# Attention a: matmuls of pairs of heads, and a GpSimd mask by minimum times 2^62

## The reference, cut to what matters

```python
topk = max(1, int(Tx * 0.3))                       # 76 of 256 keys
scores = jnp.einsum('bhid,bhjd->bhij', q, k) * scale   # 16 heads of 8
topk_scores, indices = jax.lax.top_k(scores, topk)
masked = jnp.full_like(scores, -jnp.inf).at[bi, hi, ti, indices].set(topk_scores)
attn = jax.nn.softmax(masked, axis=-1)
out = jnp.einsum('bhij,bhjd->bhid', attn, v)
```

## Time and profile before

| | |
|---|---|
| median of 3 runs | 5576.79 us (5576.01 to 5579.73) |
| profiled execution | 5576.97 us, span 5575.2 us |
| TensorE matmul busy | 5186.2 us (93%), 34686 instructions |
| VectorE busy | 4103.8 us (74%) |
| ScalarE busy | 3163.3 us (57%) |
| GpSimd busy | 2558.4 us (46%) |
| mean granted TensorE clock | 0.816 of 2.4 GHz |

### The profile page before, as it was taken

How to read it: one execution, slowest core, us unless ns; L and a number is a source line. 1 busy time by engine, 2 the same in 40 slices (tenths; PEclk the granted TensorE clock), 3 DMA queues, 4 the chain that set the end, 5 groups by cost and what they waited for, 6 DMA issues and landing times. The chain is left out here.

```text
span 5575.2 us, 122336 instructions
## 1 busy us (share of the span) xinstructions
PE 5186.2 (93%) x34686; PEld 3325.6 (60%) x34686; DVE 4103.8 (74%) x14487; ACT 3163.3 (57%) x10145; POOL 2558.4 (46%) x3026
## 2 busy tenths in 40 slices
PE   4699999999997999999989999989999999999998
PEld 3344444444443444444458888866666666788887
DVE  3788888888878888888748888855554554788886
ACT  3577777777776777777512222247766776222222
POOL 1466665665655665665534444421111111444444
PEclk6666666666666666666579999999999999999999
DMA  2000000000000000000023434310000000444344
GB/s 66 10 13 10 10 13 10 13 10 9 13 10 10 10 13 9 13 10 10 7 47 82 86 81 87 79 35 11 11 10 10 12 10 8 88 81 86 82 85 99
DMA packets 358603, 188.74 MB, mean 34 GB/s; under 512 B 190691, under 2 KB 346886, under 8 KB 358150
## 3 DMA queue, kind: packets, MB, share of 16 engines
q1 hardware_dynamic: 358150, 183.55, 16.3%
HBM read 147.04 MB, written 11.01 MB: 28 GB/s over the span
## 5 line engine op out<-in xcount | busy, mean ns | idle before, releaser
L831 ACT ACTIVATE junk<-SS,nt 128x256 bf16<-128x256 f32 x3072 | 1515.8, 499 | 79.7 <-DVE SS L946 45.1
L496 POOL TENSOR_SCALAR gone<-SS,mid 128x256 bf16<-128x256 f32 x1024 | 1228.6, 1200 | 457.4 <-DVEq L1024 326.0
L1188 POOL TENSOR_TENSOR f_hid<-f_g_m,f_cbs 128x256 f32<-128x256 f32 x1024 | 743.6, 726 | 850.5 <-DVE f_g_m L1433 661.7
L1288 ACT ACTIVATE f_th<-bank 128x256 f32<-128x256 f32 x1088 | 417.0, 383 | 1146.7 <-PE bank L1219 1146.7
L668 PE MATMUL bank<-q4x,k4x 32*128 32x256 f32 x2048 | 999.1, 579 | 0.0
L641 PE MATMUL bank<-k,q 32*128 32x256 f32 x2048 | 803.9, 584 | 40.6 <-DVE SS L946 40.6
L688 PE MATMUL bank<-pT,vaug 128*32 128x256 f32 x2048 | 830.3, 553 | 0.5 <-ACT pT L817 0.5
L1218 PE MATMUL bank<-f_xTf,wgT 128*128 128x256 f32 x2176 | 691.8, 400 | 52.6 <-DVE f_g_m L1433 37.0
L1834 DVE TENSOR_REDUCE nmxb<-bank 128x2 f32<-128x512 f32 x512 | 330.1, 688 | 475.5 <-PE bank L1606 475.5
L817 ACT ACTIVATE pT<-bank 128x512 f32<-128x512 f32 x512 | 301.4, 589 | 628.8 <-PE bank L675 626.1
L1219 PE MATMUL bank<-f_xTf,wuT 128*128 128x256 f32 x2176 | 650.9, 381 | 0.0
(11 more groups left out here) (233 smaller groups left out, 8295.7 us busy)
## 6 DMA issues: line engine op xcount, KB each, us to landing
f_cbs<-f_shares SPq DMA_DIRECT2D x512, 256.0 KB, 5.8
q4x<-q SPq DMA_DIRECT2D x64, 256.0 KB, 2.3
k4x<-k SPq DMA_DIRECT2D x64, 128.0 KB, 2.1
qrow<-q_rows SPq DMA_DIRECT2D x512, 8.0 KB
q_rows<-qTb SPq DMA_DIRECT2D x32, 128.0 KB, 1.7
out_dram<-xres SPq DMA_DIRECT2D x4, 1024.0 KB, 9.3
q4x<-nmx_rows SPq DMA_DIRECT2D x128, 4.0 KB
f_shares<-f_combT SPq DMA_DIRECT2D x64, 32.0 KB, 1.4
```

The lines of the kernel that those rows point to most:

```text
L496: last = pool.tensor_scalar(gone[:, h % 4, i, :], SS[:, (u - lag) % 4, c, :], mid[:, (u - lag) % 4, c:c + 1], FAR, ALU.is_lt, ALU.mult)
L831: nc.scalar.activation(junk[:, c % 2, :], SS[:, uu % 4, c, :], ACT.Sign, bias=bias(c), accum_out=acc[:, k, uu % 4, c:c + 1]).then_inc(s["s ...
L1188: pool.tensor_tensor(hid[:, e % NBUF, :], g_m[:, e % NBUF, :], cbs[:, par, e, :], ALU.mult).then_inc(s["hid"], 1)
```

## The change

TensorE's loop over eight places becomes a loop over four pairs of heads. `PAIRS` replaces `stage`: pairs 0 to 2 are heads 2 and 3, 4 and 5, 6 and 7 of group t-3, pair 3 is heads 0 and 1 of group t-2. For each half the pair's two masks come first, then the scores of two heads (2d+2 and 2d+3; none for pair 3), then both heads' remove. After both halves comes the work of M0 or M1, then `weigh` of the same pair, alternating between its heads. ScalarE makes the two exponentials of a pair together, at every second place. pT has four buffers instead of two, and `pv` counts pairs.

GpSimd computes min(score - mid, 0) instead of (score < mid) times 1e20, and the diagonal that TensorE multiplies with is 2^62 instead of -1. GpSimd masks two heads before the second `move` and two behind it (three and none before). `gram`, `qtok` and `mom` go from bank M1 to M0, `ktok` is made in the even step, `oT` goes to M1. `normalise` moves from place 6 to place 0 of the next step, `check_flags` from 3 to 4.

```diff
-        USES = ({"v": 0, "xT": -1, "q0": -1, "q1": -1, "k": -1, "qn": -1, "oT": 2},
-                {"f0": 1, "n0": 2, "ktok": -1, "qtok": -1, "f1": 1, "gram": -1, "mom": -1, "n1": 1, "y": 2})
+        USES = ({"v": 0, "xT": -1, "q0": -1, "q1": -1, "k": -1, "qn": -1, "gram": -1, "qtok": -1, "mom": -1},
+                {"f0": 1, "ktok": -1, "n0": 2, "oT": 2, "f1": 1, "y": 2, "n1": 1})
...
+        PAIRS = ((3, 2), (3, 4), (3, 6), (2, 0))
...
-                                last = pool.tensor_scalar(gone[:, h % 4, i, :], SS[...], mid[...], FAR, ALU.is_lt, ALU.mult)
+                                last = pool.tensor_scalar(gone[:, h % 4, i, :], SS[...], mid[...], 0.0, ALU.subtract, ALU.min)
...
-                    outsiders(2, (0, 1, 2))
+                    outsiders(2, (0, 1))
                     if runs(t):
                         move(1, "u2", nt[:, 0, :], nt[:, 1, :])
+                    outsiders(2, (2, 3))
                     if not even and ahead:
                         guess(bb + 1, (par + 1) % 2)
-                    outsiders(2, (3, 4, 5))
+                    outsiders(2, (4, 5))
...
+                    for d in range(4):
+
+                        late, a = PAIRS[d]
+                        g, v = t - late, (u - late) % 4
+                        ahead = d < 3 and runs(t, -1)
+                        n = 2 * d + 2
                         if ahead:
-                            free_bank(t + 1, h + 2)
+                            free_bank(t + 1, n + 1)
+                        if runs(g):
+                            wait(pe, s["turned"], TURNED * (g + 1))
+                            wait(pe, s["pt"], 8 * g + a)
+                        for k in range(2):
+                            if runs(g):
+                                below_max(v, a, k)
+                                below_max(v, a + 1, k)
+                            if ahead:
+                                score(n, u + 1, k)
+                                score(n + 1, u + 1, k)
+                            if runs(g):
+                                if k == 0:
+                                    wait(pe, s["out"], 8 * g + a + 2)
+                                remove(a, k)
+                                remove(a + 1, k)
...
```

`weigh` and the exponentials:

```diff
-                        wait(pe, s["pt"], 8 * g + h + 1)
+                        wait(pe, s["pt"], 8 * g + h + 2)
...
+                            for n in (h, h + 1):
+                                last = nc.tensor.matmul(O[PAD32 * (n % 4):PAD32 * (n % 4 + 1), (n // 4) * T:(n // 4 + 1) * T],
+                                                        vaug4[:, v // 2, k, 8 * (v % 2) + n, :], pT[:, n % 4, k, :],
+                                                        start=(k == 0), stop=(k == HALVES - 1), tile_position=(0, PAD32 * (n % 4)))
...
-                    wait(act, s["pv"], 8 * g + h - 1)
+                    wait(act, s["pv"], 4 * g + h // 2 - 1)
...
-                        if h == HALF:
-                            exponentials(t - 3, 7)
+                        if h % 2 == 1:
+                            late, a = PAIRS[h // 2]
+                            exponentials(t - late, a)
+                            exponentials(t - late, a + 1)
```

More of the change, by code:

```diff
@@ L495, in outsiders @@
                                 c = 2 * h + i
-                                last = pool.tensor_scalar(gone[:, h % 4, i, :], SS[:, (u - lag) % 4, c, :], mid[:, (u - lag) % 4, c:c + 1], FAR,
-                                                          ALU.is_lt, ALU.mult)
+                                last = pool.tensor_scalar(gone[:, h % 4, i, :], SS[:, (u - lag) % 4, c, :], mid[:, (u - lag) % 4, c:c + 1], 0.0,
+                                                          ALU.subtract, ALU.min)
                             last.then_inc(s["out"], 1)
@@ L627, in _ @@
                 wait(pe, s["m0c"], 5)
-                for n, f in enumerate((k_rows, q_rows, moments, spreads)):
-                    f(n)
+                k_rows(0)
+                wait(pe, s["m1c"], 1)
+                for n, f in enumerate((moments, q_rows, spreads)):
+                    f(5 + n)
                 def rows(h):
@@ L674, in remove @@
                             o = PT[h % 2][:, k * T + i * P:k * T + (i + 1) * P]
[L675 removed]
+                            last = nc.tensor.matmul(o, gone[:, h % 4, i, k * P:(k + 1) * P], steep[:, :], start=False, stop=(i == HALVES - 1))
                         if k == HALVES - 1:
@@ L739, in step @@
                         if even:
[L740 removed]
+                            if d == 0 and runs(bb, 0, BATCH):
                                 values(m0_before(bb, "v"))
[L742 to L758 removed]
@@ L759, in step @@
-                        if h == 2 and runs(t, 2):
-                            judged()
-                        if h == 5 and runs(t, 3):
-                            turn_sums()
-                        if hh >= 2:
-                            weigh(g, v, hh - 2)
-                        elif hh == 0:
-                            weigh(t - 3, (u + 1) % 4, 7)
+                            if d == 1:
+                                if runs(t, 2):
+                                    judged()
+                                if front:
+                                    turn_x(bb + 1, m0_before(bb, "xT"))
@@ new lines, in step @@
+                            if d == 2 and front:
+                                project(1, m0_before(bb, "q1"))
+                                k_rows(m1_before(bb, "ktok"))
+                            if d == 3 and runs(t, 3):
+                                turn_sums()
+                        else:
+                            if d == 0:
+                                if tail:
+                                    turn_o()
+                                if front:
+                                    wait(pe, s["m1c"], m1_before(bb, "ktok") + 1)
+                                    moments(m0_before(bb, "gram"))
+                            if d == 1:
+                                if runs(t, 2):
+                                    judged()
+                                if front:
+                                    spreads(m0_before(bb, "mom"))
+                            if d == 2 and tail:
+                                project_o()
+                            if d == 3 and runs(t, 3):
+                                turn_sums()
@@ new lines, in step @@
+                        weigh(g, v, a)
+                        if even and front:
+                            if d == 1:
+                                project(0, m0_before(bb, "q0"))
+                            if d == 2:
+                                project(2, m0_before(bb, "k"))
+                            if d == 3:
+                                queries(m0_before(bb, "qn"))
+                        if not even and front and d == 0:
+                            wait(pe, s["m0c"], m0_before(bb, "qn") + 1)
+                            q_rows(m0_before(bb, "qtok"))
@@ L922, in _ @@
                 normed(0)
-                for n, f in enumerate((take_k, take_qr, take_g)):
-                    f(n)
-                take_mom(0, 3)
+                take_k(0)
+                take_g(5)
+                take_qr(6)
+                take_mom(0, 7)
                 own.end()
```

143 lines of the change are left out of this document (50 added, 93 removed).

## The result

The changed kernel takes 5552.02 us, median of five runs (5546.77 to 5557.03), against 5576.79 (5573.89 to 5579.73): a ratio of 0.9956, 95% interval 0.9945 to 0.9968. That is faster by 0.4%, about 25 us. The forecast was faster by 147 us. The sign is right, the size is not: most of the gain that TensorE's saved work was to bring did not come.

The account below looks back on a forecast made before the run. TensorE, mostly at half clock, bounds attention a: its 105 us of half-clock work in two steps becomes 89, taking 78 instead of 81.9. Steps save 115, end 30, start 3: 5577 to 5430 us, range 5330 to 5600.

Parts of the forecast that it names:

- part 1: TensorE's masks and scores in pairs, two deep in two row tiles: 2.55 us a half, 3.8 us saved a step.
- Part 2: TensorE's weigh in pairs: two weighs in 2.14 us (1.84 to 2.60), saving 6.1 us a step (4.3 to 7.3).
- Part 3: New waits of TensorE, for the score bank and for the exponentials: 2.2 and 1.5 us in two steps.
- (a): Pair 0's free_bank waits for VectorE's copy of head 0, masks queued behind it: 1.1 us a step.
- (b): weigh waits for its own pair's two exponentials, mostly covered by work between: 1.5 us in two steps, ScalarE in time.
- rival A: VectorE alone is last, clock stays up in both steps: 75.7 us in two steps, 5361 in all; chance 20%.
- Part 4: Other engines: VectorE's floor 75.7 us in two steps, up to 78.2 with a new wait; GpSimd's mask stays at 1.20.
- The feared 2.5 us for gram: Odd step, take_g at h = 1: VectorE waits 2.5 us for TensorE's moments at half clock, none at full.
- The forecast's own 35 for these four steps: Last four steps, without scores: 39 us each become 28, the first two held at 37 and 30; 35 us saved.
- B: ScalarE late to its two exponentials, TensorE and VectorE slip: 81 us in two steps, 5517 in all; chance 12%.
- C: Waits keep the clock at half in both steps: 89 us in two steps, 5753 in all; chance 14%.
- D: Four masks and scores together in 1.16 us instead of 2.01, VectorE then last: 5361 in all; chance 4%.

Follow-up runs that it names:

- e8: Changed kernel with masks reading the rows of the head two further on, so a pair's masks and scores use four row tiles (wrong data): 5445.89 us, ratio 0.9758.
- e10: e4 with weigh taking one head after the other instead of alternating between the two: 5376.55 us, ratio 0.9676.
- e2: Changed kernel with each pair's masks and remove put ahead of the bank wait and scores: 5389.84 us, ratio 0.9661.
- e4: Changed kernel with both edits, masks ahead of the bank wait and weigh one pair later: 5372.69 us, ratio 0.9632.
- e6: Changed kernel with masks ahead of the bank wait in pair 0 alone: 5532.60 us, ratio 0.9909.
- e11: e4 with q4x and k4x stored turned by 64 partitions (eight DMAs a step, not four), giving masks other row tiles with right data: 5373.40 us, ratio 0.9675.
- e7: Kernel before with one wait moved: place 0 already waits for the bank that place 1 needs: 5660.15 us, ratio 1.0137.
- e3: Changed kernel with weigh moved one pair later, behind the next pair's masks: 5482.31 us, ratio 0.9822.
- e5: Kernel before with the second half of each weigh left out (part of the result missing): 5575.34 us, ratio 0.9993.
- e1: Kernel before with the GpSimd mask alone changed to min(score - mid, 0) and the diagonal to 2^62: 5561.82 us, ratio 0.9970.

## Why the prediction was right and wrong

**What bounds, and part 1: right.** A pair's half is two deep in two tiles, as the last fence but one of the first section shows: 1085.96 to 1087.97 is 2.01, and 0.54 to the next mask. 2.55 was forecast. The last pair, masks alone, takes 1.16 + 0.54, as forecast:

```profile
1157.88 1.23 PE L668 MATMUL bank<-q4x,k4x 32*128 32x256 f32 x4
1159.04 0.61 PE L675 MATMUL bank<-steep,gone 128*128 128x128 bf16 x4
1159.58 1.23 PE L668 MATMUL bank<-q4x,k4x 32*128 32x256 f32 x4
```

Reading rows(h) and not the change's words was right: there are no four row tiles. The Trainium skill, "TensorE: Matmul & The Clock Gate", section "Part 3: Packing small matmuls — row/col tiling", shows tiles of different row groups overlapping; e8, which puts masks and scores in four of them, agrees, 1.17 us instead of 2.01.

**Part 2: right, on the cheap side.** Two weighs go in 1.86 at half clock (2.14 forecast, 1.84 the lower bound), so they lie fully side by side:

```profile
1136.39 1.92 PE L689 MATMUL bank<-pT,vaug 128*32 128x256 f32 x8
1138.25 0.71 PE L611 MATMUL bank<-wqT_a,xT 128*128 128x128 f32 x2
```

By e10 it was worth nothing where VectorE is last.

**Part 3: the step that failed.** It put the new waits at 2.2 + 1.5 = 3.7 us in two steps. TensorE idles for 16: 7.9 ahead of the masks (SS and the row named DMA, 93.3 us over 11.9 pairs of steps), 3.9 ahead of the weigh, 2.5 for osum, 1.0 for q, 0.4 for onrm. Not all of that is loss: e2 and e4 leave TensorE idle for 15.3 and 14.5 us and are faster, because there VectorE is last. What the two waits cost stands in the period: 82.86 us becomes 76.79 with the bank wait moved, 79.31 with the weigh moved, 75.61 with both. Together that is 7.3 us, where the forecast of 78 stood 2.3 above VectorE's floor. Three errors lie in it. First, (a) was counted at pair 0 alone, "a step's start", though two of three banks a pair make it the case at every pair with scores; e6 shows that mending pair 0 alone brings 19 of 162 us. Second, its price was that of a copy, with VectorE taken to stand ready. VectorE is itself 69 of 83 us busy, has its loop's end of 3.46 us, and comes when it comes; the longest wait is 7.2. Third, (b) rested on the argument that ScalarE is there in time because it waits in the earlier trace rows. But it waits in order, too. TensorE stood 2.31 us for this one:

```profile
1103.92 0.38 ACT L796 ACTIVATE xT<-bank 128x256 f32<-128x256 f32 x1 [3.81 <-PE bank L574]
...
1104.66 0.51 ACT L798 ACTIVATE xTc<-xT,xsum 128x256 f32<-128x256 f32 x1
1105.08 1.06 ACT L831 ACTIVATE pT<-bank 128x512 f32<-128x512 f32 x2
```

The exponentials were ready to go when remove was done, but ScalarE stood in take_x, waiting for TensorE's turn_x, which comes behind them. A queue with idle time is no proof that it will be there: what it idles for may be ahead of what is needed.

The sentence "Behind it queue the masks, although they need no bank" is in the prediction. I saw the mechanism and priced it as one copy and two semaphores. With TensorE's busy time of 66.9 us and the forecast 3.7 of waits, two steps would have been 71, below VectorE's floor, and rival A's time would have come; e4 is that case, and e2 comes near it.

**Part 4: right in the number, in part by luck.** 75.7 us was VectorE's floor (e4: 75.61 in its fast run, e10 and e11 76.0 and 76.3). rinv is gone from its waits, as forecast. prod is not: its 1.4 us in two steps stand in after and e4 as before (15.9 and 17.3 us, with `issue` for TensorE as the name), and in after ktok is new with 18.5 us. In turn the waits of zt behind flags, which the prediction did not count, fell from 17.9 to 6.0 us. The feared 2.5 us for gram are 0.2 at most. GpSimd's mask keeps its price, 1138 ns in the middle where 1142 was; the prediction's 1.20 is the mean, which the earlier trace rows do not show:

```profile
L493 POOL TENSOR_SCALAR gone<-SS,mid x1024: 1130/1138/1696, 173.6 to 2799.3; 128x256 bf16<-128x256 f32 x171
```

**The sum.** Steps: -115 forecast, +9.7 measured. End: -30 forecast, -42.8 measured; there pairs without scores have no bank to wait for, which is my reading of why the end alone got the gain. It fits e7: its wait stands only where scores are made, and its end takes 152.1 us, as before's. The forecast's own 35 for these four steps should have been 33 (2, 9 and twice 11). Start: -3 forecast, +2.9 measured.

Where the clock rises was forecast wrong, though the mean came near (0.57 to 0.60 forecast, 0.62 measured). It was to rise in the even step, with the odd one mostly at half. In these two pairs of steps of after, even and odd in turn, the even ones have 0.58 and 0.61 and an odd one has 0.78:

```profile
1077.50:1122.00 44.50, 32.29 (x144) 18.80 (x144) 34.74 (x135) 27.13 (x102) 23.29 (x27) 0.58 0.06 10
1122.00:1162.10 40.10, 36.93 (x172) 20.96 (x170) 33.80 (x134) 31.47 (x113) 23.45 (x28) 0.58 0.06 11
1162.10:1201.90 39.80, 29.84 (x143) 16.71 (x143) 34.72 (x136) 28.26 (x105) 23.76 (x27) 0.61 0.06 11
1201.90:1241.20 39.30, 31.79 (x190) 18.15 (x190) 33.99 (x134) 34.03 (x126) 25.66 (x30) 0.78 0.06 11
```

The steps were to take 38 and 40 us; these take 44.5, 40.1, 39.8 and 39.3.

**The rivals.** B came nearest: waits that don't hide, 81 us in two steps forecast for it, 82.9 measured, and 5517 against 5552. But the wait that it names, ScalarE late to the exponentials, is the smaller part (e3, 70 us); the larger, for the bank (e2, 162 us), it does not have. A chance of 12% was low for a change that puts a wait for ScalarE into every pair and one for VectorE into three of four. Its "against" (ScalarE busy 61 of 82) was the same error as (b). C's condition, full clock for under 9% of the time, did not arise: the mean is 0.62, 24% at full. D's arrangement, made in e8, gave 5446 and not 5361: the waits held it too.

## What to carry to other kernels

When an edit groups work in pairs, look at what each wait is for and put it directly ahead of the one instruction that needs it, with all independent work of the group in front; here the wait for the copies takes 93 us of 983 ahead of the masks and 80 ahead of the scores, and two steps take 82.9 and 76.8. Price a wait on another engine by where that engine is at that moment in its own queue, not by the duration of what is waited for, and count it at every place where the buffers run short. Work taken off the busiest engine pays only so far as buffers let it run ahead, and the engine that comes next is where to read the limit: here VectorE's, about 76 us a pair of steps.

## What the runs showed of the hardware

- TensorE's granted clock can take back saved work without a new wait: e5 is 96% busy as before, with a sixth less work, at 0.57 instead of 0.67. And waits need not lower it: e4 leaves TensorE idle for 19% of the window at 0.67, the same as before with 4% idle. The Trainium skill, "TensorE: Matmul & The Clock Gate", section "HAM oscillation — how this bites in real kernels", has it that sustained matmuls bring the full rate and waits lose it; the means of these kernels do not show it.
- Two steps take 81.92 us in before and again in e6, whose TensorE has 22% less work and other waits. Only the means agree: before's pairs of steps take 81.9 each, e6's between 80.0 and 84.0.
- Four fp32 matmuls over 32 rows each, in four row tiles, start within 0.02 us and are through in 1.17 us at half clock; two tiles two deep take 2.01.
- The kernel before, unchanged, has a median of 5558.8 us on one chip and 5575 to 5577 on the others. A difference of 0.3% between kernels that were not measured on one chip says nothing here, and e1's on one chip says little. The change's own 0.4%, though measured beside before on one chip, is hardly more.
